# A graph network's two edge pipelines: softplus in one VectorE operation, its constant moved into the next product's bias

## The reference, cut to what matters

```
filter  = ssp(edge_attr_20 @ W_f1 + b_f1) @ W_f2 + b_f2      # per edge, times edge_weight
message = (x @ W_in2f)[src] * filter                         # summed by destination
update  = ssp(y @ W_o1 + b_o1) @ W_o2 + b_o2                 # per node, added to x
```

## Time and profile before

| | |
|---|---|
| median of three runs | 2582.02 us (2577.95 to 2592.12) |
| span of the profiled execution | 2583.3 us, 46,833 instructions |
| TensorE (PE) busy | 2195.1 us, 85% |
| VectorE (DVE) busy | 1965.6 us, 76% |
| ScalarE (ACT) busy | 1777.9 us, 69% |
| GpSimd (POOL) busy | 1640.3 us, 63% |
| mean granted TensorE clock | 0.938 |

### The profile page before, as it was taken

How to read it: one execution, slowest core, us unless ns; L and a number is a source line. 1 busy time by engine, 2 the same in 40 slices (tenths; PEclk the granted TensorE clock), 3 DMA queues, 4 the chain that set the end, 5 groups by cost and what they waited for, 6 DMA issues and landing times. The chain is left out here.

```text
span 2583.3 us, 46833 instructions
## 1 busy us (share of the span) xinstructions
PE 2195.1 (85%) x14558; PEld 1832.7 (71%) x14558; DVE 1965.6 (76%) x2833; ACT 1777.9 (69%) x3703; POOL 1640.3 (63%) x1214
## 2 busy tenths in 40 slices
PE   4999999999998899999896898988788888487464
PEld 4889888998887677776664777777566666376454
DVE  5888888998896566668775899977588888487454
ACT  4788887888786577776664777766588888465221
POOL 5877756676730533427885556688557776588787
PEclk9999999999999999998888999999899999788776
DMA  3555554555555888878886677778647777576653
GB/s 102 134 151 139 129 141 136 152 147 137 139 159 162 227 258 252 251 209 216 206 218 167 137 168 173 165 206 215 180 135 203 198 199 202 125 159 163 170 158 100
DMA packets 336934, 444.74 MB, mean 172 GB/s; under 512 B 120943, under 2 KB 177093, under 8 KB 336690
## 3 DMA queue, kind: packets, MB, share of 16 engines
q1 hardware_dynamic: 216386, 377.83, 51.9%
q0 software_dynamic: 120000, 63.45, 14.0%
q10 hardware_dynamic: 304, 0.49, 0.1%
HBM read 251.01 MB, written 191.28 MB: 171 GB/s over the span
## 5 line engine op out<-in xcount | busy, mean ns | idle before, releaser
L1711 POOL DMA_INDIRECT acc<-combined,first_ x100 | 212.0, 2120 | 123.0 <-DMA acc<-combined,first_ 85.5
L452 PE MATMUL banks<-mats,g_hT 128*125 128x256 f32 x1000 | 259.5, 382 | 0.0
L472 PE MATMUL banks<-mats,g_zT 128*125 128x128 f32 x2000 | 239.2, 273 | 0.2
L472 PEld LDWEIGHTS banks<-mats,g_zT 128*125 128x125 f32 x2000 | 228.4, 188 | 0.5 <-issue 0.3
L746 POOL DMA_INDIRECT gin_xs<-x,from_ x100 | 125.2, 1252 | 162.0 <-DMA x_of_src<-gin_xs 138.0
L589 DVE TENSOR_REDUCE g_ss<-g_sq 125x4 f32<-125x1024 f32 x125 | 151.5, 1212 | 90.5 <-ACT g_sq L516 64.9
L516 ACT ACTIVATE g_sq<-banks 125x512 f32<-125x512 f32 x250 | 145.2, 593 | 101.8 <-PE banks L452 72.2
L452 PEld LDWEIGHTS banks<-mats,g_hT 128*125 128x125 f32 x1000 | 189.6, 190 | 27.1 <-issue 0.4
L381 POOL DMA_INDIRECT g_xd<-in_x,idx x100 | 129.2, 1292 | 116.8 <-PE banks L487 90.1
L533 ACT ACTIVATE g_zT<-banks,cols 128x500 f32<-128x500 f32 x250 | 179.0, 775 | 13.6 <-PE banks L460 7.9
L1771 POOL DMA_INDIRECT combined<-acc,idx x100 | 142.4, 1424 | 58.2 <-PE banks L1882 28.3
(11 more groups left out here) (390 smaller groups left out, 7068.4 us busy)
## 6 DMA issues: line engine op xcount, KB each, us to landing
x<-g_x SPq DMA_DIRECT2D x125, 224.0 KB
g_x<-in_xT SPq DMA_DIRECT2D x100, 250.0 KB
acc<-g_zero SPq DMA_DIRECT2D x101, 224.0 KB
gin_x<-x SPq DMA_DIRECT2D x50, 448.0 KB
h<-gin_hr SPq DMA_DIRECT2D x50, 448.0 KB
al_h<-h SPq DMA_DIRECT2D x40, 448.0 KB
al_x<-x SPq DMA_DIRECT2D x40, 448.0 KB
out<-al_out SPq DMA_DIRECT2D x40, 448.0 KB
```

Of the source, the lines that this page charges most:

```text
L452: m = nc.tensor.matmul(bank[0:P, 256 * j:256 * j + 256], HT[q % 2][:, c:c + P], K.W1c, start=False, stop=j == 1)
L472: m = nc.tensor.matmul(pO[q % 2][0:P, D * j:D * j + D], ZT[q % 2][:, h, P * j:P * j + P], K.W2[:, h, :], start=False, stop=j == R - 1 and ...
L1711: pool.indirect_dma_start(out=K.acc, out_offset=bass.IndirectOffsetOnAxis(ap=K.first[:, g, r:r + 1], axis=0), in_=CR[:, g, r * D:r * D + D ...
```

## The change

`max(z, 0) + log(...) - log 2` is written as `max(product, -bias) + log(...)` plus the column `bias - log 2`. The column is the same for every edge, so the product behind the softplus turns it into a constant: `W_f2.T @ (b_f1 - log 2)` is added to b_f2 (`bf2s`), and `(b_o1 - log 2) @ W_o2` to the row b_o2, of which `bias_u` is built anew. The negated biases are kept in `nbf1` and `nbo1`. All Relu and `positive` operations go, with their semaphores; `soft` reads pG itself; and the product that next writes pG waits for the `soft` before it. A new class `Prepared` makes the constants once, at the start of `gin`, in three pieces between that stage's own operations, and `back` of the third group waits for the last of them, since it uses the same bank.

```diff
+class Prepared:
...
+    def on_tensor(self, pe, n):
+        if n == 0:
+            pe.wait_ge(self.made, 3)
+            nc.tensor.matmul(bank[:, 320:448], self.wide[:, :], K.W("o2"), start=True, stop=True)
+            nc.tensor.matmul(bank[:, 304:305], K.W("f2"), self.rest[:, 0:1], start=True, stop=True).then_inc(self.told, 1)
+    def on_vector(self, dve, n):
+        nc, K, bank = self.nc, self.K, self.bank
+        if n == 0:
+            self.link(dve, nc.vector.tensor_scalar(self.rest[:, 0:1], K.c("bf1"), LOG2, None, ALU.subtract))
+            self.link(dve, nc.vector.tensor_scalar(self.rest[:, 1:2], K.c("bo1"), LOG2, None, ALU.subtract))
+            self.link(dve, nc.vector.tensor_scalar(self.wide[:, :], K.ident[:, :], 0.0, self.rest[:, 1:2], ALU.mult, ALU.add))
+        elif n == 1:
+            dve.wait_ge(self.told, 1)
+            self.link(dve, nc.vector.tensor_tensor(K.bf2s[:, :], bank[:, 304:305], K.c("bf2"), ALU.add))
+            self.link(dve, nc.vector.tensor_tensor(self.row[:, :], bank[:, 320:448], K.bo2_rows[:, :], ALU.add))
+            self.link(dve, nc.vector.tensor_scalar(K.nbo1[:, :], K.c("bo1"), -1.0, None, ALU.mult))
+            self.link(dve, nc.vector.tensor_scalar(K.nbf1[:, :], K.c("bf1"), -1.0, None, ALU.mult))
+        else:
+            self.link(dve, nc.vector.tensor_copy(self.part[0][:, :], self.row[:, :]))
+            self.link(dve, nc.vector.tensor_tensor(self.rest[:, :], self.row[:, :], self.part[0][:, :], ALU.subtract))
+            self.link(dve, nc.vector.tensor_copy(self.part[1][:, :], self.rest[:, :]))
+            self.link(dve, nc.vector.tensor_tensor(self.row[:, :], self.rest[:, :], self.part[1][:, :], ALU.subtract))
+            self.link(dve, nc.vector.tensor_copy(self.part[2][:, :], self.row[:, :]))
+            wide = K.bias_u[:, :].rearrange("p (r d) -> p r d", r=R)
+            part = [p[:, :].rearrange("p (o d) -> p o d", o=1).to_broadcast([128, R, D]) for p in self.part]
+            self.link(dve, nc.vector.tensor_scalar(wide, part[0], K.ident[:, 0:1], None, ALU.mult))
+            for i in (1, 2):
+                self.link(dve, nc.vector.scalar_tensor_tensor(out=wide, in0=part[i], scalar=K.ident[:, i:i + 1], in1=wide,
+                                                              op0=ALU.mult, op1=ALU.add))
 # gin, TensorE: back(q)
+                    if q == 2:
+                        pe.wait_ge(pr.made, 15)
 # gin, TensorE's and VectorE's turns
+                    if i in (0,):
+                        pr.on_tensor(pe, i // 2)
+                    if i in (0, 1, 3):
+                        pr.on_vector(dve, (i + 1) // 2)
 # edges_first
                 def first(k):
-                    past(pe, rl, k - 1)
+                    past(pe, sp_, k - 1)
-                def positive(k):
-                    nc.scalar.activation(SP[k % 2][:, :], pG[:, 0:G], ACT.Relu, bias=K.c("bf1")).then_inc(rl, 1)
                 def soft(k):
-                    past(dve, rl, k)
                     past(dve, l1, k)
-                    nc.vector.scalar_tensor_tensor(out=SP[k % 2][:, :], in0=SP[k % 2][:, :], scalar=LOG2, in1=AB[k % 2][:, :],
-                                                   op0=ALU.subtract, op1=ALU.add).then_inc(sp_, 1)
+                    past(dve, wp, k - 2)
+                    nc.vector.scalar_tensor_tensor(out=SP[k % 2][:, :], in0=pG[:, 0:G], scalar=K.nbf1[:, :], in1=AB[k % 2][:, :],
+                                                   op0=ALU.max, op1=ALU.add).then_inc(sp_, 1)
 # edges_middle (soft_d likewise, with l1d, updd, SPD, ABD, spd)
                 def first(k):
-                    past(pe, rld, k - 1)
-                    past(pe, abd, k - 1)
+                    past(pe, spd, k - 1)
                 def first_d(k):
-                    past(pe, rl, k)
-                    past(pe, ab, k)
+                    past(pe, sp_, k)
-                def positive(k):
-                    nc.vector.tensor_scalar(SP[k % 2][:, :], pG[:, 0:G], K.c("bo1"), 0.0, ALU.add, ALU.max).then_inc(rl, 1)
                 def soft(k):
+                    past(dve, l1, k)
                     past(dve, upd, k - 2)
+                    nc.vector.scalar_tensor_tensor(out=SP[k % 2][:, :], in0=pG[:, 0:G], scalar=K.nbo1[:, :], in1=AB[k % 2][:, :],
+                                                   op0=ALU.max, op1=ALU.add).then_inc(sp_, 1)
```

More of the change, by code:

```diff
@@ L146, in setup @@
     K.same = keep("same", [128, E + 1], BF16)
+    K.bf2s, K.nbo1, K.nbf1 = [keep(n, [128, 1]) for n in ("bf2s", "nbo1", "nbf1")]
     idx = keep("idx", [P, 3, EG, R], I32)
@@ L690, in _, with __init__, link @@
                            (-4, "edge", sums)])
+class Prepared:
+    def __init__(self, nc, K, bank, ctx):
+        self.nc, self.K, self.bank = nc, K, bank
+        self.made, self.told = K.sem("pr_made"), K.sem("pr_told")
+        self.count = 0
+        self.wide, self.row, self.rest = [ctx.enter_context(nc.sbuf_tensor(f"pr_{n}", [128, 128], F32)) for n in ("wide", "row", "rest")]
+        self.part = [ctx.enter_context(nc.sbuf_tensor(f"pr_part{i}", [128, 128], BF16)) for i in range(3)]
+    def link(self, dve, ins):
+        self.count += 1
+        ins.then_inc(self.made, 1)
+        dve.wait_ge(self.made, self.count)
+    def on_tensor(self, pe, n):
[5 more added lines that the diff above has]
+    def on_vector(self, dve, n):
+        nc, K, bank = self.nc, self.K, self.bank
+        if n == 0:
[20 more added lines that the diff above has]
+                                                              op0=ALU.mult, op1=ALU.add))
@@ L1612, in _ @@
                 bn.on_scalar(act)
-                steps(EG, [(1, na.log_of(act)), (1, lambda k: na.exp(act, k, rm)), (0, relu_b), (3, keep_c), (0, size), (0, positive),
+                steps(EG, [(1, na.log_of(act)), (1, lambda k: na.exp(act, k, rm)), (0, relu_b), (3, keep_c), (0, size),
                            (1, copy_x2), (0, expo), (2, rows_m), (0, lambda k: na.square(act, k, flat(A[k % 2]), a)), (0, log)])
@@ L1653, in weights @@
                     past(dve, mt, k - 2)
[L1654 removed]
+                    nc.vector.scalar_tensor_tensor(out=WT[k % 2][:, :], in0=pW[:, 0:G], scalar=K.bf2s[:, :], in1=EW[k % 4][:, :],
                                                    op0=ALU.add, op1=ALU.mult).then_inc(wt, 1)
@@ L1799, in edges_middle @@
         kept_s, kept_d, kept_x, kept_t = [sem_list(K, f"em_{n}", 3) for n in ("kept_s", "kept_d", "kept_x", "kept_t")]
-        (hT, bt, yT, yt, ydT, ydt, back, a, x2, o1, ab, e1, l1, rl, sp_, o1d, abd, e1d, l1d, rld, spd, upd, b, x3, updd, bd, x3d,
+        (hT, bt, yT, yt, ydT, ydt, back, a, x2, o1, ab, e1, l1, sp_, o1d, abd, e1d, l1d, spd, upd, b, x3, updd, bd, x3d,
          x3T, xt, x3dT, xdt, u, ht, scan, me, ud, htd, bk, hr, bkd, hrd, cs, c, done) = [sem(n) for n in (
-            "hT", "bt", "yT", "yt", "ydT", "ydt", "back", "a", "x2", "o1", "ab", "e1", "l1", "rl", "sp", "o1d", "abd", "e1d", "l1d",
-            "rld", "spd", "upd", "b", "x3", "updd", "bd", "x3d", "x3T", "xt", "x3dT", "xdt", "u", "ht", "scan", "me", "ud", "htd",
+            "hT", "bt", "yT", "yt", "ydT", "ydt", "back", "a", "x2", "o1", "ab", "e1", "l1", "sp", "o1d", "abd", "e1d", "l1d",
+            "spd", "upd", "b", "x3", "updd", "bd", "x3d", "x3T", "xt", "x3dT", "xdt", "u", "ht", "scan", "me", "ud", "htd",
             "bk", "hr", "bkd", "hrd", "cs", "c", "done")]
@@ L2062, in apply_a, with soft, soft_d @@
                     nc.vector.tensor_tensor(A[k % 2][:, :, :], A[k % 2][:, :, :], na.times(k), ALU.mult).then_inc(x2, 1)
-                def positive(k):
-                    past(dve, ab, k)
+                def soft(k):
+                    past(dve, l1, k)
                     past(dve, upd, k - 2)
-                    nc.vector.tensor_scalar(SP[k % 2][:, :], pG[:, 0:G], K.c("bo1"), 0.0, ALU.add, ALU.max).then_inc(rl, 1)
[L2069 to L2076, removed]
-                    past(dve, updd, k - 2)
[L2078 to L2084, removed]
+                    nc.vector.scalar_tensor_tensor(out=SP[k % 2][:, :], in0=pG[:, 0:G], scalar=K.nbo1[:, :], in1=AB[k % 2][:, :],
+                                                   op0=ALU.max, op1=ALU.add).then_inc(sp_, 1)
+                def soft_d(k):
+                    past(dve, l1d, k)
+                    past(dve, updd, k - 2)
+                    nc.vector.scalar_tensor_tensor(out=SPD[k % 2][:, :], in0=pG[:, 0:G], scalar=K.nbo1[:, :], in1=ABD[k % 2][:, :],
+                                                   op0=ALU.max, op1=ALU.add).then_inc(spd, 1)
                 def join(k):
@@ L2134, in apply_c @@
                     nc.vector.tensor_tensor(C[k % 4][:, :, :], C[k % 4][:, :, :], nc_.times(k), ALU.mult).then_inc(done, 1)
-                steps(EG, [(1, apply_b), (1, nbd.reduce_of(dve)), (0, residual), (1, apply_bd), (1, sums), (0, positive), (1, average),
```

(3 more changed lines are left out.)

9 lines of the change are left out of this document (4 added, 5 removed).

## The result

The changed kernel takes 2645.28 us (median of four runs, 2644.17 to 2651.5); the kernel before, on the same chip, 2584.14 (the three runs of above and one more, 2577.95 to 2592.12). The ratio is 1.0245, with an interval of 1.0216 to 1.0275: slower by 61 us. Forecast were 2653 and a range of 2620 to 2681.

A forecast was written before the change was run, and what follows sets the result against it. No engine alone was taken to bound edges_middle; a chain round three engines set its 13.76 us step. 2583.3 + 43 + 22 + 1.5 + 4 = 2653.8 us, against the median 2653; range 2620 to 2681.

The forecast's parts named there:

- The wait and its place: edges_middle: first_d would wait for soft, start 1.9 us later, and leave TensorE a hole of about 2.1 us each step.
- The serial chain: edges_middle: logarithm, soft and first_d, which overlapped, run one after the other; +1.70 us a step, +43 us, bounds 0 to +57.
- The clock: edges_middle: the hole lowers TensorE's clock in 14 of 25 steps at 1.6 us, +22 us; bounds 0 and +40.
- A fall on every pass: edges_middle: the rival in which the clock falls in every step, +40 us, total 2671 us; chance 0.19.
- rival A: edges_middle: the serial chain without a lower clock; with the small terms +48.5 us, total 2630 us; chance 0.27.
- VectorE's saved work: edges_middle: 36 us of VectorE busy time go with the two maxima; counted as 0 on the path, other end -36.
- rival C: edges_middle: VectorE is the bound, so the change makes the kernel faster, total 2554 us; chance 0.04.
- edges_first: edges_first: soft reads the bank, +0.06 us a step over 25 steps, +1.5 us; bounds 0 and +5.
- gin: gin: 15 small VectorE operations and two products that make the constants, partly hidden, +4 us once; bounds 0 and +7.

The follow-up runs named there:

- e2: The kernel before, with one wait added: first_d in edges_middle also waits for soft of its own turn; 2617.2 us, ratio 1.0377 to the kernel before.
- e1: The changed kernel with the source path's maximum in edges_middle taken early again, so first_d waits for that and not for soft; 2518.31 us, ratio 0.9985.
- r1: The changed kernel itself, run once more in another set; 2603.86 us, ratio 1.0257 to the kernel before.
- e3: The changed kernel with nine unused 512-column products per turn ahead of first_d in edges_middle; 2569.56 us, ratio 1.0173 to the kernel before.
- e5: The changed kernel with four unused 512-column products per turn ahead of first_d in edges_middle; 2579.35 us, ratio 1.0142 to the kernel before.
- e8: The kernel of e1 (changed kernel, source maximum early again) in a second set of runs; 2528.19 us, ratio 0.9955 to the kernel before.
- e7: The changed kernel with both maxima in edges_middle early again, source and destination path; 2539.27 us, ratio 1.0001 to the kernel before.
- r2: The kernel before itself, unchanged, run once more for its trace beside r1; 2545.31 us (one run).
- e4: The changed kernel with back_h and second ahead of first_d, and the two norm operations and copy_x3d ahead of size_d, in edges_middle; 2550.11 us, ratio 1.0112.
- e6: The kernel of e1 with the eight operations that build bias_u moved from gin to the start of edges_first; 2527.7 us, ratio 0.9955 to the kernel before.
- e9: The kernel of e6 run again in another set, beside e8; 2518.6 us, ratio 0.9921 to the kernel before.

## Why the prediction held, step by step

**The wait and its place: right.** em_sp ends the hole before first_d, 2.24 us where about 2.1 were forecast, and size_d starts 1993.31 - 1991.12 = 2.19 us after the logarithm ahead of it, 0.05 before: 2.1 us later, where 1.9 were forecast. e2 and e1 show it from both sides.

**The serial chain: right in size.** +1.70 us a turn forecast, 14.92 - 13.13 = 1.79 measured between clean turns. The hand-over from soft to first_d is 1992.04 - 1991.89 = 0.15 us, not the 0.07 assumed; the rest fits.

**The clock: right in mechanism, too small.** Forecast 14 of 25 turns at 1.6 us = +22; measured 18 of 24 at 1.67 = +30, and +32 with what else lengthens those turns. The price was read well from the earlier trace rows. The share was a guess between holes of 1.73 and 2.33 us; with 2.24 it was 18 of 24, and 16 of 24 in r1. A fall on every pass would have given 40 us; the measurement lies between that and my value. The Trainium skill ("TensorE: Matmul & The Clock Gate", section "HAM oscillation — how this bites in real kernels") tells of such a fall on every pass in a kernel whose waits last about 3 to 5 us. The prediction left that length out; with holes of 2.24 us this case has the fall in most turns and not in all.

**The step that failed: the sum was built on a clean turn and added to a mean one.** The +1.70 came from a turn of 13.17 us and was added 25 times to a span whose turns are 13.76 on the mean. The 0.6 us between them stood in the earlier trace rows and I passed over it. The longer turns swallowed those stops: -15 us by the account above. e3 and e5, which are rival A (the chain without a lower clock), show it: first to last em_a is 357.6 and 358.2 us in them, against 330.2 and 323.4 in the two executions of the kernel before, so 27 to 35 us more and not 43. In the whole time they stand 47 and 37 us above the kernel before, where 48.5 were forecast for A.

**VectorE's saved work: 0 on the path, right for this version.** Summed over its grouped rows VectorE has 33.0 us less in edges_middle (the two maxima of 36.1 went, the two softs grew from 33.6 to 36.7), as forecast. In e1 the like saving, of half the size, shows up in the time, since there it is not behind a wait: 0.2 us a turn and the stops. I had held rival C, VectorE as the bound, for a question of yes or no; the list does bind a little, and the wait hid that. One reading under C was off too: in the earlier trace rows soft ends at 2030.64, 2.5 us after TensorE had finished turn_x3d (2028.38 - 0.25), not 1.9. The 1.9 belongs to a soft that is moved up. No term of the sum used it.

**edges_first: 0 instead of +1.5.** ef_a to the next stage's first row is 237.1 and 237.2 us. The +0.06 us a step is too small to see here: over all profiled executions this distance was 233.1 to 241.4 us.

**gin: +6.4 instead of +4**, within the bounds of 0 to 7. Timeline of the kernel after:

```profile
848.14 0.22 DVE L730 CAST pr_part<-pr_row 128x128 bf16<-128x128 f32 x1
...
850.34 1.54 DVE L739 SCALAR_TENSOR_TENSOR bias_u<-pr_part,ident,bias_u 128x512 bf16<-128x512 bf16 x2
...
851.91 0.68 DVE L957 COPY gin_xT<-banks 128x500 f32<-128x500 f32 x1
...
852.65 1.94 PE L877 MATMUL banks<-gin_xT,mats 128*128 128x500 f32 x2 [2.74 <-DVE gin_xT L957]
```

The eight operations take 3.74 us (3.3 estimated) and hold up the copy at 851.91. TensorE waits 2.74 us and then works at the lower clock: two products in 1.94 us, which took 1.01 in the earlier trace rows. Over eight profiled executions with all of `Prepared` in gin the stage took 334.1 to 338.5 us, and 329.3 to 330.3 in three without it.

So the time was met, to 0.3%, in part by luck, with errors of both signs: the clock 10 us too small, the stops 15 us not seen, gin 2 too small, other stages 7 us lower.

## What to carry to other kernels

An operation that reads its input twice, early and late, can hold a buffer for much less time than the one that fuses both. Before fusing, look who waits for that buffer: if two pipelines share a bank, the last read of one is the start of the other, and saving 0.7 us of a busy engine cost 1.8 us of chain. Where whoever needs the buffer has to wait for the last step anyway, as on the path of the destinations, fuse: that half of the change brought 0.5% here (e8 against e7), the other half cost 2.6 to 3.0% (the kernel after against e1 and e8, each by its ratio).

And measure a turn over many: if the mean is above the cleanest one, find out what the difference is before a sum rests on either.

## What the runs showed of the hardware

- A hole of 2.24 us in each turn of about 15 us lowered TensorE's clock in 18 of 24 turns and in 16 (r1), one of 2.67 us (e2) in 21; one of 1.44 us (e5) and 0.35 us (e3) made none of the 24 turns a slow one. Nine unused products of 512 columns made the kernel faster: ratio 1.0173, where the kernel after had 1.0245 and 1.0257.
- Which of the turns are spared is not regular (after the first turns the quicker ones stand singly, between two to five slow ones), and I found no reason in the rows.
- The stops, turns longer by 0.7 to 2.2 us, come in 7 to 10 of 24 turns wherever VectorE has its full list in a 13.13 us turn (before, r2, e7), and none of that size in e1, e3, e4, e5, e6, e8, e9 and the kernel after, though single turns there are 0.5 us longer. In the first profile every second turn has one, from the fourth to the 22nd; in the others the order is less even. What ends them is not in the rows: the releaser named had long been done. Their cause is open, and so is the reason for the 7 us that stages without a change gave back in the first profile.
- The kernel before takes 2522.9, 2542.6 or 2540.4 us (medians of 13, 12 and 23 runs) in the sets of the experiments, and 2584.1 in the first: 2.4%. The clean turn was 13.13 us in both of its profiles. In the two that were profiled the difference lies ahead of the change: gin's first product starts at 843.4 us in the first profile and at 809.6 in the second (r2), 34 of the 40 us between their spans.
